# A two-layer vision tower: the first attention with its features in rows (half of the batch, feature), residual in the content stage, and a stationary output matrix in the second attention

## What is computed

```python
h = h + _L0_attn_ref(_layernorm(h), ...)   # the first attention, changed here
h = h + _L0_ffn_ref(_layernorm(h), ...)    # mixture of experts
h = h + _L1_attn_ref(...)                  # a linear recurrence
h = h + _L1_ffn_ref(h, ...)                # rope attention with 4 heads, then experts
```

## Time and profile before

| | |
|---|---|
| time, median of 3 runs | 1231.48 us (1221.51, 1231.48, 1232.14) |
| the profiled execution | 1219.27 us, its span 1217.5 us |
| mean granted TensorE clock | 0.937 of 2.4 GHz |
| busy: TensorE, its loads, VectorE, ScalarE, GpSimd | 1081.6, 811.2, 879.7, 608.3, 458.1 us |

### The profile page before, as it was taken

One profiled execution on the slowest core, in us unless ns is written; L12 is line 12 of the kernel. 1 busy time (PEld: TensorE's weight loads), 2 busy tenths in 40 slices (PEclk: granted clock), 3 DMA queues, 4 the chain that ended last, 5 costly groups with the idle time before them and its releaser, 6 DMA issues. The chain is left out here.

```text
span 1217.5 us, 23980 instructions
## 1 busy us (share of the span) xinstructions
PE 1081.6 (89%) x8420; PEld 811.2 (67%) x8420; DVE 879.7 (72%) x2104; ACT 608.3 (50%) x1269; POOL 458.1 (38%) x613
## 2 busy tenths in 40 slices
PE   6795877959999999997588969988799999999996
PEld 2464776746777777775474547768687777777774
DVE  1696656966777777775678769973677888877874
ACT  2254774636556655653324437770554454554552
POOL 2373001211434434434326478730033433333334
PEclk8797999969999999999698989995799999999998
DMA  8100000000000000000000000000000000000000
GB/s 246 83 1 1 2 1 2 1 1 1 2 1 1 1 1 2 1 1 1 1 1 1 1 1 3 2 3 1 1 7 6 7 6 7 6 12 6 7 7 12
DMA packets 3455, 13.57 MB, mean 11 GB/s; under 512 B 400, under 2 KB 2192, under 8 KB 2960
## 3 DMA queue, kind: packets, MB, share of 16 engines
q1 hardware_dynamic: 3056, 8.00, 2.3%
q0 software_dynamic: 288, 4.11, 0.9%
HBM read 9.97 MB, written 2.13 MB: 10 GB/s over the span
## 5 line engine op out<-in xcount | busy, mean ns | idle before, releaser
L1306 PE MATMUL moe_psU<-moe_nT_parts,moe_w_hi 128*128 128x320 f32 x988 | 325.4, 340 | 1.7 <-ACT moe_nT_parts L1048 0.9
L1306 PE MATMUL moe_psU<-moe_nT_parts,moe_w_lo 128*128 128x320 f32 x988 | 297.4, 311 | 0.0
L1306 PEld LDWEIGHTS moe_psU<-moe_nT_parts,moe_w_hi 128*128 128x128 f32 x988 | 188.5, 191 | 56.6 <-issue 50.1
L1306 PEld LDWEIGHTS moe_psU<-moe_nT_parts,moe_w_lo 128*128 128x128 f32 x988 | 189.1, 191 | 0.0
L1210 DVE TENSOR_TENSOR moe_hid<-moe_psU,moe_silu 128x320 f32<-128x320 f32 x286 | 139.4, 491 | 62.3 <-ACT moe_silu L1074 52.6
L1001 POOL TENSOR_TENSOR moe_sum<-moe_scaled 128x256 f32<-128x256 f32 x130 | 99.1, 763 | 171.1 <-DVE moe_scaled L1200 170.5
L1074 ACT ACTIVATE moe_silu<-moe_psU 128x320 f32<-128x320 f32 x286 | 125.5, 439 | 56.5 <-PE moe_psU L1306 39.2
L1079 ACT ACTIVATE moe_hid<-moe_psU,middle 128x320 f32<-128x320 f32 x260 | 129.5, 528 | 34.1 <-PE moe_psU L1306 31.8
L126 POOL TENSOR_TENSOR moe_stats<-moe_stats,minus_half 128x5 f32<-128x5 f32 x26 | 31.5, 1213 | 274.6 <-DVE moe_stats L1123 274.6
L1216 DVE TENSOR_SCALAR moe_hid<-moe_psU,middle 128x320 f32<-128x320 f32 x156 | 85.7, 550 | 67.5 <-PE moe_psU L1306 66.7
L1317 PE MATMUL moe_psY<-moe_hid,middle 128*64 128x320 f32 x832 | 124.8, 442 | 0.7 <-ACT moe_hid L1079 0.7
(11 more groups left out here) (301 smaller groups left out, 1982.5 us busy)
## 6 DMA issues: line engine op xcount, KB each, us to landing
images<-in_x SPq DMA_DIRECT2D x8, 576.0 KB, 11.0
late<-in_late POOLq DMA_DIRECT2D x1, 2456.5 KB, 12.5
out_tokens<-h SPq DMA_DIRECT2D x13, 160.0 KB, 1.8
middle<-in_middle POOLq DMA_DIRECT2D x1, 1554.0 KB, 7.4
early<-in_early SPq DMA_DIRECT2D x1, 1042.5 KB, 18.8
early<-in_early SPq DMA_DIRECT2D x1, 80.0 KB, 2.0
```

What stands on the lines that cost most here:

```text
L1306: last = pe.matmul(psum[:, 0:HALF], w[:, col:col + SPLIT], moving, start=(part == 0), stop=(part == 1))
```

## The change

**Layout.** The second layer is four products of 64 rows by 64 columns per tile instead of one 128x128 product in two pieces. Its result lies as [128, 2, 320]: partitions 0 to 63 belong to samples 0 to 63, partitions 64 to 127 to samples 64 to 127, and keys and queries are the two planes. `phi` becomes [128, 2, 65*64]. The second tanh becomes two instructions, one for each plane, since their biases differ. In content0 a group is four samples of each half, the features lie in all 128 partitions, and `kf` and `qf` exist twice (`features(i)` waits for scores(i-2), not (i-1)). A score product reads 64 rows and alternates between the upper and the lower half of the array; an output product has 64 columns and alternates between the left and the right half; `keep_outputs` is one instruction of 128 partitions. `psO` exists twice. In combine0 `contents` makes two 64x64 products per token.

**Moves.** The residual (two GpSimd instructions per tile) leaves project0 and stands in content0, 13 tiles one after the other from the stage's start. The norm is kept in `n_all` for it. The first two `take_norm` now stand ahead of the chain of angles, and `cs_diag` is made in 13 pieces inside the loop (`turn_back`).

**output1.** `wo1` (128x64) is the stationary operand and the activations are the moving one, two tiles of tokens at a time side by side in columns 0 to 63 and 64 to 127; ScalarE copies the result, TensorE transposes it (five per pair), VectorE adds it to x and GpSimd adds x to h.

The core of the diff:

```diff
...
                 pool.memset(first[:, 0:1], 0.0).then_inc(first_set, 1)
                 for g in range(NT):
                     rstd_step(pool, stats[g % 3], minus_half, rstd_asked, rstd, g + 1)
-                    if g >= 2:
-                        add_norm(g - 2)
-                add_norm(NT - 2)
-                add_norm(NT - 1)
...
-                    act.activation(tanh2[g % 2][:, :], psB[:, 0:TOK], ACT.Tanh, bias=early[:, c["bkq2"]]).then_inc(tanh2_set, 1)
+                    for x in range(2):
+                        ins = act.activation(tanh2[g % 2][:, x, :], psB[:, x, :], ACT.Tanh, bias=early[:, c["bkq2"]][:, x:x + 1])
+                    ins.then_inc(tanh2_set, 1)
...
-                    for begin, n in pieces():
-                        last = pe.matmul(psB[:, begin:begin + n], early[:, c["wkq2"]], tanh1[g % 2][:, begin:begin + n],
-                                         start=True, stop=True)
+                    hidden = tanh1[g % 2][:, :].rearrange("p (t b) -> p t b", b=B)
+                    for half in range(2):
+                        for x in range(2):
+                            rows = slice(D * x, D * x + D)
+                            last = pe.matmul(psB[D * half:D * half + D, x, :], early[rows, c["wkq2"]][:, rows],
+                                             hidden[rows, :, HALF_B * half:HALF_B * half + HALF_B], start=True, stop=True)
...
             @block.gpsimd
             def _(pool):
-                pool.memset(kf[64:, :, :], 0.0).then_inc(c_blank, 1)
-                pool.memset(qf[64:, :, :], 0.0).then_inc(c_blank, 1)
                 pool.memset(val[64:, :, :], 0.0).then_inc(c_blank, 1)
                 pool.memset(score[64:, :, :], 0.0).then_inc(c_blank, 1)
+                pool.wait_ge(c_blank, 2)
+                for g in range(NT):
+                    need(pool, added, g)
+                    tokens = slice(g * T, (g + 1) * T)
+                    pool.tensor_tensor(n_all[:, tokens, :], n_all[:, tokens, :],
+                                       early[:, c["bo0"]].unsqueeze(1).to_broadcast([B, T, D]), ALU.add).then_inc(moved_set, 1)
+                    pool.wait_ge(moved_set, g + 1)
+                    pool.tensor_tensor(h[:, tokens, :], h[:, tokens, :], n_all[:, tokens, :], ALU.add).then_inc(added, 1)
+                pool.wait_ge(added, NT)
...
-                act.wait_ge(c_ang, 1)
-                act.activation(cs[:, :], ang[:, :], ACT.Sin).then_inc(c_cs, 1)
 
                 def features(i):
-                    need(act, c_S, i)
-                    for rows, dst in ((slice(0, 64), kf), (slice(64, 128), qf)):
-                        act.activation(dst[0:64, :, :].rearrange("p b t -> p t b"), batches(phi, i, rows), ACT.Sin,
-                                       bias=early[rows, c["sin_bias"]], scale=early[rows, c["sin_scale"]]).then_inc(c_feat, 1)
+                    need(act, c_S, i - 1)
+                    for x, dst in enumerate((kf, qf)):
+                        act.activation(dst[i % 2][:, :, :].rearrange("p b t -> p t b"), group(x, i), ACT.Sin,
+                                       bias=early[:, c["sin_bias"]], scale=early[:, c["sin_scale"]]).then_inc(c_feat, 1)
...
                 features(0)
-                act.wait_ge(c_blank, 4)
+                features(1)
+                act.wait_ge(c_blank, 2)
                 values(0)
-                features(1)
+                act.wait_ge(c_ang, 1)
+                act.activation(cs[:, :], ang[:, :], ACT.Sin).then_inc(c_cs, 1)
...
                 def scores(i):
                     pe.wait_ge(c_feat, i * 2 + 2)
                     need(pe, c_score, i * 2)
-                    for b in range(BG):
-                        last = pe.matmul(psS[:, b // HB, (b % HB) * L:(b % HB + 1) * L], kf[:, b, :], qf[:, b, :],
-                                         start=True, stop=True)
+                    for j in range(HB):
+                        for half in range(2):
+                            rows = slice(D * half, D * half + D)
+                            last = pe.matmul(psS[:, half, j * L:(j + 1) * L], kf[i % 2][rows, j, :], qf[i % 2][rows, j, :],
+                                             start=True, stop=True)
                     last.then_inc(c_S, 1)
 
                 def outputs(i):
                     pe.wait_ge(c_val, i + 1)
                     pe.wait_ge(c_score, i * 2 + 2)
-                    need(pe, c_out, i)
-                    for b in range(BG):
-                        last = pe.matmul(psO[:, b // HB, (b % HB) * L:(b % HB + 1) * L], val[:, b, :], score[:, b, :],
-                                         start=True, stop=True)
+                    need(pe, c_out, i - 1)
+                    for j in range(HB):
+                        for half in range(2):
+                            b = half * HB + j
+                            last = pe.matmul(psO[i % 2][D * half:D * half + D, j * L:(j + 1) * L], val[:, b, :], score[:, b, :],
+                                             start=True, stop=True)
                     last.then_inc(c_O, 1)
 
                 values(0)
...
-                chain.link(dve.tensor_copy(ang[:, :], early[:, c["phase"]]))
-                reduced_angle(dve, chain, ang[:, :], turns[:, :], early[:, c["quarter"]], early[:, c["half_pi"]])
-                dve.sem_inc(c_ang, 1)
-                dve.wait_ge(c_tanh, 1)
-                dve.tensor_scalar(gates[:, 0, :], th[:, :], 0.5, 0.5, ALU.mult, ALU.add).then_inc(c_tab, 1)
-                dve.tensor_scalar(gates[:, 1, :], th[:, :], -0.5, 0.5, ALU.mult, ALU.add).then_inc(c_tab, 1)
...
+                def angles():
+                    chain.link(dve.tensor_copy(ang[:, :], early[:, c["phase"]]))
+                    reduced_angle(dve, chain, ang[:, :], turns[:, :], early[:, c["quarter"]], early[:, c["half_pi"]])
+                    dve.sem_inc(c_ang, 1)
+                    dve.wait_ge(c_tanh, 1)
+                    dve.tensor_scalar(gates[:, 0, :], th[:, :], 0.5, 0.5, ALU.mult, ALU.add).then_inc(c_tab, 1)
+                    dve.tensor_scalar(gates[:, 1, :], th[:, :], -0.5, 0.5, ALU.mult, ALU.add).then_inc(c_tab, 1)
+
+                def turn_back(k):
+
+                    if k == 0:
+                        dve.wait_ge(c_cs, 1)
+                        chain.link(dve.tensor_tensor(cs_norm[:, :], cs[:, :], early[:, c["pos_norm"]], ALU.mult))
+                    tokens = slice(k * T, (k + 1) * T)
+                    dve.tensor_tensor(cs_diag[:, tokens, :], early[:, c["stack2"]].unsqueeze(1).to_broadcast([128, T, D]),
+                                      cs_norm[:, tokens].unsqueeze(2).to_broadcast([128, T, D]), ALU.mult).then_inc(c_tab, 1)
 
...
                 def keep_outputs(i):
                     dve.wait_ge(c_O, i + 1)
-                    for k in range(2):
-                        out = phi[0:64, :].rearrange("p (t b) -> p b t", b=B)[:, bass.ds(i * BG + k * HB, HB), :]
-                        last = dve.tensor_copy(out, psO[:, k, 0:HB * L].rearrange("s (b t) -> s b t", t=L))
-                    last.then_inc(c_out, 1)
+                    dve.tensor_copy(group(0, i).rearrange("p t b -> p b t"),
+                                    psO[i % 2][:, 0:HB * L].rearrange("s (b t) -> s b t", t=L)).then_inc(c_out, 1)
 
                 take_norm(0)
                 take_norm(1)
-                dve.wait_ge(c_blank, 4)
+                angles()
+                dve.wait_ge(c_blank, 2)
                 for i in range(0, NBG - 2):
                     weigh_scores(i)
                     take_norm(i + 2)
+                    if 1 <= i <= NT:
+                        turn_back(i - 1)
                     keep_outputs(i)
...
-                        last = pe.matmul(psC[0][:, k, :], content[:, (t0 + k) * B:(t0 + k + 1) * B], ident[:, 0:D],
-                                         start=True, stop=True)
+                        for half in range(2):
+                            rows = slice(D * half, D * half + D)
+                            last = pe.matmul(psC[0][rows, k, :], phi[rows, 0, (t0 + k) * HALF_B:(t0 + k + 1) * HALF_B],
+                                             ident[rows, rows], start=True, stop=True)
...
 
         with nc.Block() as block:
             @block.tensor
             def _(pe):
-                for g in range(NT):
-                    need(pe, x_set, g - 3)
+                def project(k):
+                    g, n = PAIRS[k]
+                    need(pe, sides_set, k - 1)
+                    for begin, cols in pieces():
+                        for s in range(n):
+                            at = (g + s) * TOK + begin
+                            last = pe.matmul(psA[k % 2][D * s:D * s + D, begin:begin + cols], late[:, c["wo1"]],
+                                             yT[:, at:at + cols], start=True, stop=True)
+                    last.then_inc(A_mm, 1)
+
+                def turn(k):
+                    rows = D * PAIRS[k][1]
```

(35 more changed lines are left out.)

91 lines of the change are left out of this document (36 added, 55 removed).

## The result

The changed kernel takes 1192.57 us, the median of four executions (1186.37 to 1195.69), beside 1230.66 for the kernel before (1221.51 to 1232.14, four). The ratio is 0.9704, with a 95% interval of 0.9652 to 0.9755: about 3.0% faster. Measured again later with six executions it was 1188.23, ratio 0.9684 (0.9627 to 0.9742). The forecast was 1192, in a range of 1175 to 1214. The medians of the two sets differ by 38.1 and 41.2 us; the two profiled executions, 1219.27 and 1186.37 us, each among the fastest of their kernel, differ by 32.9.

A forecast was written before the change was run, and what follows sets the result against it. Bounds: VectorE in combine0 and five project0 periods, waits in content0's loop, TensorE in output1. Savings 5 + 0 + 15.3 + 1.0 + 0.5 + 11.5 = 33.3 us gave 1186.0 (profile) or 1198.2 (median); middle 1192, range 1175 to 1214.

The forecast's parts named there:

- project0: Stage project0: unstretched phi and norm plus a second layer of 1.1 us bring TensorE's period to 3.75; 5 us saved.
- the estimate from psY: project0's second layer: records overlap two at a time, as the experts' psY records do, so it costs 1.1 us.
- The start of content0: Content0 up to the first mask: table leaves the path, linked angle steps slow down; first mask as before, 0 us.
- The collision: Content0's start: each linked angle step waits out a GpSimd addition, 8.5 us instead of 3.7; without it, 5.7 us saved.
- The loop: Content0, first mask to last: five groups at 3.1, ten at 2.6, plus 2 us; 43.5 against 58.8, saving 15.3.
- the ring: Content0's loop: O, ScalarE's copy of the values, V, then O again wait on each other; 2.5 us, taken as 2.6.
- combine0: Stage combine0: quarter-array products are covered by VectorE, only the first tiles can gain; 0.5 us saved.
- output1: Stage output1: long records raise the clock, TensorE takes 1.75 us per pair of tiles; 11.5 us saved.
- row halves do not overlap: Rival, chance 0.15: second layer takes 2.34 us and S 1.1 in the loop; 16.3 us saved, 1209.
- no pair overlaps: Rival, chance 0.06: project0 +9, content0 -9 at 3.2 per group, output1 -5; 1220, no change.
- drain at a change of row half: Rival, chance 0.05: the array loses 0.16 us at each change of row half; slower, 1243 to 1255.
- Four tiles overlap: Half of a rival, chance 0.18, with additions not colliding: 1184 without collision, 1180 with four tiles overlapping too.

The follow-up runs named there:

- the first experiment: Changed kernel, but GpSimd starts content0's residual additions only once the two gates are made; 1183.36 us, ratio 0.9655 to the kernel before.

## Why the prediction held, point by point

**The sum.** The mechanisms named for the stages are the ones that the traces show, with the exceptions told below. But that 1192 lies 0.6 us from the first median and 4 from the second is in part luck. The sum of 33.3 us meets the 32.9 between the profiled executions because project0 gained 2.3 us more and output1 2.4 less than foreseen. And the medians differ by 38.1 and 41.2 us, 5 to 8 more than the sum; 1192 fits since it is the middle between the sum taken from the profiled execution (1186.0) and from the median (1198.2). Where these 5 to 8 us lie is open, since only one execution of the kernel before was profiled.

**project0.** Expected -5, measured -7.3. The mechanism was right, `phi` and norm at their short values throughout. One term was too large: the second layer takes 0.70 instead of 1.1, the estimate from psY. With it TensorE needs 3.83 - 1.17 + 0.70 = 3.36 and VectorE, back to back at 3.55, bounds instead of TensorE's 3.75. VectorE's own need had been put 0.19 too low. The 0.70 lies near the low end of 0.58: the records run in fours and not in pairs. The Trainium skill, "TensorEngine Tiling (Array Packing)", section Tiling Modes, has four tiles in 64x64 mode and says that tiles operate independently; the trace agrees for this one shape, with four records starting within 0.02 us. Of what the four tiles gain over pairs, 0.4 us per tile, VectorE's 3.55 lets the stage have 0.2.

**The start of content0.** Expected 0, with the first mask 13.2 us after the barrier; measured 13.2. The nine steps and two gates took 9.1 us (106.35 to 115.44) against 9.6. They began 4.2 instead of 3.6 us after the barrier, because each of the two norm copies ahead of them costs 1.1 and not 0.65. Two errors of half a microsecond cancel here. The collision, seen before the change only in single instructions, was the right reading, and the first experiment shows what an undisturbed start is worth: the rival's 5.7 us, measured 6.5.

The Trainium skill, "SBUF — State Buffer", section SBUF: two separate sides, gives the exclusive lock on the shared port pair to a VectorE instruction in a 2-port mode or with two SBUF inputs, or to a GpSimd instruction, whichever starts first. The traces agree for mask and keep, which have one input in PSUM and stay at 0.74 to 0.76 and 0.59 to 0.62 beside GpSimd, and for the table pieces, which have two inputs in SBUF and go from 0.48 to up to 1.17. The norm copy, from SBUF to SBUF, depends on its pattern: it is stretched with runs of eight (0.65 to 1.28, in the kernel with the residual moved alone) and with the token innermost (0.77 to 1.39), and not with runs of four (1.07 to 1.13 either way).

**The loop.** Expected 43.5, measured 42.7. Period 2.57 to 2.73 against 2.6, O 0.62 against 0.6, the ring O, copy, V as named. Two terms behind it were wrong without showing in the time. The features take 0.85 and 0.80, not 0.77, and leave the path without their second buffer, which the prediction held to be needed. VectorE's sum was put at 2.3 and hidden; it is 2.56, since the norm copy was taken over from the earlier trace rows at 0.65 although the change gives it another access pattern, at 1.10. It is a second limit at the same height as the ring, which the prediction did not see; the experiments had to lift both. The first five groups were foreseen at 3.1 each plus 2 in all, together 17.5. The masks show 16.0, and another shape: 3.15, 5.03, 2.42, 2.98 and 2.44. In the second group V at the low clock (2.02), norm copy, the scaling of the angles and the first table piece stand one behind the other.

**combine0.** Expected -0.5, measured 0. Its length differs by up to 14 us between executions of kernels that carry the same combine0 (73.6 to 87.3 us), so this term can't be told from zero. That both main profiles have 73.6 was not foreseen from anything, and the agreement of the sum rests on it.

**output1.** Expected 16.1 us to its end, a gain of 11.8 by its own lines that the sum carries as 11.5; measured 18.76 (798.98 to 817.74), and 19.9 to the experts. The mechanism holds: the clock rises, TensorE alone bounds. The pair costs 1.93 instead of 1.75: the products 1.22 for 1.17, and the five transposes 0.70 for 0.58, 0.14 each where the price of the columns alone gives 0.12; seven times 0.18 is 1.3 us. The low clock costs 2.6 instead of 2.0: the first two products and the first transposes took 5.7 us, where 1.22 + 1.22 + 0.70 = 3.1 would do. The rest, 0.8, is the tail: GpSimd's last two additions stand one behind the other, 2.35 us from 815.38, where one of 1.0 was foreseen. This profile is on the slow side: the stage took 17.1 to 18.8 us to the experts in the eleven other profiles of this stage, ten of them 18.6 to 18.8, with the first transposes already at the high clock in the kernel that has output1 alone (0.77 us instead of 1.33).

**The rivals.** Row halves overlap (S 0.62, second layer 0.70), so "row halves do not overlap" and "no pair overlaps" are out. No drain at a change of row half can be seen: S changes rows at each sample and takes no longer than O, which changes columns, and the order without changes is the slower one. "Four tiles overlap" was true, for a fifth of a microsecond per tile; the other half of that rival, no collision, was not.

## What to carry to other kernels

When an instruction keeps its element count but gets another access pattern, it needs its own price: the new pattern of the norm copy cost 0.45 us per group here and made a hidden engine a limit. Two limits at the same height hide each other; lifting one shows nothing, so look at what each engine would need alone before giving up on an edit. And work moved to GpSimd is not free where VectorE runs linked short steps or SBUF copies: put it behind such a chain (here 6.5 us in the chain and 4.9 in the stage), and count what is left of it in the loop (5.4 us for 26 additions, from one profile each). Last, when stages of the same instructions differ by several microseconds between profiles, as project0's first tiles and combine0 do here, compare the periods and not the lengths of the stages.

## What was not expected of the hardware

- Eight fp32 records of 320 columns on quarters of the array take 0.70 us, 0.09 each, against 0.29 for a full one. They start in fours, within 0.02 us. Exchanging the order within the quarters changes nothing.
- A group of 16 small records gains from alternating halves even at 65 columns: 0.62 against 0.9 us. Records of different halves start 0.007 us apart when they follow each other, records of one half 0.06.
- The slowest of three access patterns of the same VectorE copy, 1.10 us for 520 elements, was the only one that GpSimd's additions did not stretch.
- With the same instructions combine0 took 74 to 87 us, by where the clock fell in it. With TensorE kept busy at the seam ahead of it, it took 73.6 in one profile and 80.6 in another.
